# Spans of 512 queries, one ring of seven PSUM banks and a gating product on Pool, in two layers of attention with experts

## The chip, the cores and the metric

One core of a Trainium2 chip. The metric is the device time of one execution in microseconds (us); the kernel before was run three times, and one more execution was profiled. Engine names are those of the profile: PE (TensorE), DVE (VectorE), ACT (ScalarE), POOL (GpSimd), SP (SyncE, which issues the DMAs).

## What is computed

`x` is (4, 1024, 128), float32. Four residual steps follow one another, each on the layer norm of `x`:

```
x = x + attention_a(norm(x))   # 16 heads of 8; softmax over all keys, then the causal mask, no renormalising
x = x + experts(norm(x))       # softmax router over 8 experts, 2 chosen, plus one shared expert
x = x + attention_b(norm(x))   # 16 heads of 8, rotary tables, full softmax, output projection and bias
x = x + experts(norm(x))       # the same weights again
```

An expert is `(silu(h @ w1) * (h @ w3)) @ w2` with all widths 128. The kernel computes all nine experts for every token and multiplies each by its gate (zero where it was not chosen). Softmax subtracts the row's maximum, so every score is computed twice: once (queries on partitions) for the maximum, once (keys on partitions, with the negated maximum as two more rows of the contraction) for the exponent.

## The kernel before, in words

Tokens lie on partitions; a batch of 1024 tokens is two chunks of 512, a chunk four tiles of 128. Attention is cut into 32 groups: layer (0 or 2, attention a or b), batch, and a set of four heads. The four heads of a group lie at partitions 0, 32, 64 and 96, so their products with a contraction of 24 or 26 rows use different rows of PE's array.

A plan, one list of items (`make_plan`), is walked by all five engines; each engine issues its part of every item in that order and waits on semaphores. `begun` is the start: projections of chunks 0 and 1, then score units with the other six projections between them. `attention` is the loop of 1024 steps, two to a block (128 keys by 512 queries by 4 heads). A step holds, in this order: the side items due at it, one score unit 46 steps ahead (`LEAD`), two exponent products and their exponentials, and half of the weighing of the block two behind. `ended` is the rest.

- A score unit (`scores`, L1114 to L1124) is two products of 512 keys into a slot of two banks, and one DVE reduction of 128x1024 (`take_max`, L912 to L917). 32 units make a group; then `combine` (L919), a transpose, a split in two limbs on POOL (`split_max`, L610) and eight small DMAs (`load_maxima`, L513) put the maxima into `qx`. The exponents of a group wait for them.
- An exponent (`exponent`, PE L1140 to L1148, ACT L751 to L761) is one product into one bank and one ACT instruction of 128x512.
- `weigh` (L1163) multiplies the exponentials by the values, in four column groups; `mask` on POOL (L625) makes the causal diagonal blocks of attention a.
- Banks: a ring of three single banks (`ONE`) for all that ACT reads, a ring of two double slots (`TWO`) for all that DVE reads, and one bank that accumulates. `bank_of` and `slot_of` (L1058, L1065) wait until the user before in the same ring is read.
- Projections: `query_or_key` (L1098), `values` (L1106), `split_qk` (L730) and `projected_a` (L121) for attention a; `queries_keys` (L1088), `rope_product` (L891) and `projected_b` for attention b. The rows go to DRAM (`store`) and come back by group (`load`, L501, eight DMAs of 96 KB on SP).
- An expert unit (one expert, one chunk; 144 in all, `feed_forward` L148) is: h1 on PE (three products, L1201), tanh and a copy on ACT (L798, L801), silu on DVE (two operands in SBUF, L961), h3 on PE, hid on DVE (L970), y on PE (L1219), a copy on ACT (L825), four scalings and one addition on POOL (`add_gated`, L638). Units come every 7 steps (`PACE`). Those of layer 1 for a batch begin 50 steps after it is done. In `ended` the unit uses Silu on ACT (L803), one DVE pass (L974), four scalings on ACT (L816) and one addition on POOL (L660).
- Before a chunk's units stand its statistics, transpose and logits (`prepared`), and before a batch's gates a chain of 19 small DVE operations on the router's logits (`chain`), eight chains in all.

## Time and profile before

| | |
|---|---|
| three runs, median (lowest to highest) | 2003.87 us (1995.84 to 2017.19) |
| the profiled execution: its time, its span | 2010.94 us, 2009.2 us |
| busy PE / DVE / ACT / POOL | 1857.0 / 1571.9 / 1447.1 / 715.7 us |
| mean granted TensorE clock | 0.944 of full speed |
| first exponential, last exponential | 137.2 us, 1919.6 us |

The span runs from the first to the last instruction. Matmuls overlap and their ends are modelled, so PE's busy time is no measure of how full it is; the stretches, waits and intervals below are read for that.

### The profile page before, as it was taken

Reading aid. Unit: us, or ns where it says so; the run is one execution under the profiler, and the core shown is the slowest. Engines: PE = TensorE matmul, PEld = TensorE weight load, DVE = VectorE, ACT = ScalarE, POOL = GpSimd, SP = SyncE. Lnnn points to the kernel's source line nnn. Section 1 sums busy time; section 2 is a strip of 40 time slices with the busy share of each in tenths; the row PEclk is TensorE's granted clock in tenths of the full one; section 3 lists DMA queues with packets and bytes.
Section 4 is the critical chain, followed back from the end, with each engine's and each line's share of the span. In section 5 each row is a group of like instructions: output and inputs, shape, how many; then the busy total and the mean of one; then the engine's idle time right before and its main releaser. Section 6 shows DMA issues by size and latency. Waiting matters only on the chain.

```text
span 2009.2 us, 42496 instructions
## 1 busy us (share of the span) xinstructions
PE 1857.0 (92%) x16784; PEld 884.3 (44%) x16784; DVE 1571.9 (78%) x2030; ACT 1447.1 (72%) x2890; POOL 715.7 (36%) x984
## 2 busy tenths in 40 slices
PE   2889999999999999999989999999998999999988
PEld 1344443444444444444444444444444444444467
DVE  3779999988969789888888888888878888887132
ACT  1238888877667776777877787776786778778765
POOL 4222223344634446444452322323222222322244
PEclk7559999999969999999999999989999999999999
DMA  5220100000100001001010010101000000000000
GB/s 178 110 111 18 46 19 18 19 17 18 49 18 16 35 18 49 18 18 41 11 48 17 17 49 18 38 13 48 17 23 18 23 13 20 10 2 8 1 6 17
DMA packets 38087, 61.79 MB, mean 31 GB/s; under 512 B 4352, under 2 KB 19328, under 8 KB 37760
## 3 DMA queue, kind: packets, MB, share of 16 engines
q1 hardware_dynamic: 37888, 59.07, 8.3%
q8 instruction: 133, 2.18, 0.5%
q14 instruction: 66, 0.54, 0.1%
HBM read 30.74 MB, written 27.26 MB: 29 GB/s over the span
## 4 chain that ended last, share of the span: by engine, by line
PE 69%; DVE 18%; ACT 6%; issue 5%; POOL 1%; DMA 1%; SPq 0%; POOLq 0%; DVEq 0%; ACTq 0%
PE ps_sum L1181 22%; PE ps_two L1124 16%; DVE negmax L915 11%; PE ps_one L1148 5%; PE ps_one L1219 5%; PE ps_two L1201 4%; PE ps_one L1201 4%; PE ps_sum L1219 3%; DVE silu L961 2%; PE ps_sum L1201 2%; PE ps_sum L1148 2%; ACT probs L760 1%; DVE xn L935 1%; PE ps_two L1095 1%; PE ps_one L1103 1%
## 5 line engine op out<-in xcount | busy, mean ns | idle before, releaser
L915 DVE TENSOR_REDUCE negmax<-ps_two 128x2 f32<-128x1024 f32 x1024 | 1223.0, 1220 | 227.8 <-PE ps_two L1124 222.7
L760 ACT ACTIVATE probs<-ps_one 128x512 f32<-128x512 f32 x1382 | 783.0, 603 | 150.6 <-PE ps_one L1148 90.4
L1124 PE MATMUL ps_two<-kx,qx 24*128 24x512 f32 x2048 | 528.9, 518 | 71.1 <-DVE negmax L915 50.9
L1148 PE MATMUL ps_one<-qx,kx 26*128 26x512 f32 x1382 | 567.6, 505 | 6.8 <-ACT first L801 4.1
L1181 PE MATMUL ps_sum<-probs,vg 128*9 128x256 f32 (+1 forms) x6144 | 474.4, 382 | 7.1 <-ACT sums L767 5.6
L760 ACT ACTIVATE probs<-ps_sum 128x512 f32<-128x512 f32 x666 | 401.6, 603 | 91.9 <-PE ps_one L1148 68.4
L1124 PEld LDWEIGHTS ps_two<-kx,qx 24*128 24x128 f32 x2048 | 194.8, 189 | 444.3 <-DVE negmax L915 194.8
L648 POOL TENSOR_SCALAR scaled<-scaled,gates 128x128 f32<-128x128 f32 x468 | 173.6, 390 | 516.8 <-ACT scaled L825 516.6
L1148 PE MATMUL ps_sum<-qx,kx 26*128 26x512 f32 x666 | 336.1, 505 | 4.4 <-ACT first L801 3.2
L1148 PEld LDWEIGHTS ps_one<-qx,kx 26*128 26x128 f32 x1382 | 216.5, 184 | 61.9 <-ACT probs L760 33.3
L627 POOL TENSOR_TENSOR pdiag<-probs,causal 128x512 f32<-128x512 f32 x128 | 166.4, 1301 | 181.5 <-ACT probs L760 181.4
L1181 PE MATMUL ps_sum<-probs,w 128*9 128x256 f32 (+1 forms) x2560 | 186.2, 363 | 3.6 <-ACT sums L767 3.3
L1181 PEld LDWEIGHTS ps_sum<-probs,vg 128*9 128x9 f32 x6144 | 99.4, 89 | 186.0 <-issue 163.3
L652 POOL TENSOR_TENSOR x<-x,scaled 128x512 f32<-128x512 f32 x117 | 151.2, 1292 | 9.7
L1148 PEld LDWEIGHTS ps_sum<-qx,kx 26*128 26x128 f32 x666 | 122.9, 185 | 28.2 <-ACT probs L760 11.7
L961 DVE SCALAR_TENSOR_TENSOR silu<-silu,first 128x512 f32<-128x512 f32 x117 | 104.0, 889 | 22.4 <-ACT first L801 22.4
L1219 PE MATMUL ps_one<-w,hid 128*128 128x128 f32 x712 | 107.7, 297 | 5.7 <-DVE hid L974 5.7
L970 DVE TENSOR_TENSOR hid<-silu,ps_two 128x512 f32<-128x512 f32 x117 | 80.2, 685 | 40.2 <-PE ps_two L1201 37.5
L1219 PEld LDWEIGHTS ps_one<-w,hid 128*128 128x128 f32 x712 | 93.7, 203 | 38.4 <-issue 15.0
L1201 PE MATMUL ps_two<-x_hi,w_hi 128*128 128x512 f32 x144 | 71.3, 495 | 18.1 <-DVE negmax L915 17.1
L825 ACT ACTIVATE scaled<-ps_one 128x512 f32<-128x512 f32 x76 | 45.4, 598 | 56.0 <-PE ps_one L1219 54.0
L615 POOL TENSOR_SCALAR mlimbs<-turned_max 32x128 fp32r<-32x128 f32 x32 | 9.2, 288 | 205.5 <-ACT turned_max L777 205.4
(153 smaller groups left out, 1883.4 us busy)
## 6 DMA issues: line engine op xcount, KB each, us to landing
qk_rows<-limbs SPq DMA_DIRECT2D x36, 512.0 KB, 3.3
qx<-qk_rows SPq DMA_DIRECT2D x128, 96.0 KB
kx<-qk_rows SPq DMA_DIRECT2D x128, 96.0 KB
qk_rows<-prod_c SPq DMA_DIRECT2D x8, 512.0 KB, 3.7
qx<-mlimbs SPq DMA_DIRECT2D x256, 4.0 KB
qk_rows<-prod_s SPq DMA_DIRECT2D x4, 512.0 KB, 2.9
out_dram<-x SPq DMA_DIRECT2D x8, 256.0 KB, 2.3
x<-in_x SPq DMA_DIRECT2D x3, 512.0 KB, 6.1
```

The costliest lines, as they stand in the source:

```text
L627: pool.tensor_tensor(m.pdiag[:, d % 2, :, :], m.probs[:, blk % PROB_SLOTS, :, at:at + P], m.causal[:, :].unsqueeze(1).to_broadcast([P, GH, ...
L648: last = pool.tensor_scalar(part, part, m.gates[:, c * CT + t, e:e + 1], 0.0, ALU.mult, ALU.add)
L652: pool.tensor_tensor(x, x, m.scaled[:, i % 2, :], ALU.add).then_inc(s.added, 1)
L760: act.activation(m.probs[:, blk % PROB_SLOTS, EXP_HEADS[k], :], bank, ACT.Exp, scale=SCALE).then_inc(s.freed[ONE], 1)
L915: dve.tensor_reduce(m.negmax[:, unit // UNITS % 2, half, first:first + NT + 1:NT], ps.rearrange("p (h k) -> p h k", h=2), AX.X, ALU.max, n ...
L961: dve.scalar_tensor_tensor(m.silu[:, k % 2, :], m.silu[:, k % 2, :], 1.0, m.first[:, :], ALU.add, ALU.mult).then_inc(s.silued, 1)
L970: dve.tensor_tensor(m.hid[:, k % 2, :], m.silu[:, k % 2, :], ps[:, 0:CHUNK], ALU.mult).then_inc(s.freed[TWO], 1)
L1124: last = pe.matmul(slot[:, bank * CHUNK:(bank + 1) * CHUNK], m.qx[rows, n % SLOTS, i * P:(i + 1) * P], m.kx[rows, n % SLOTS, half * CHUNK: ...
L1148: pe.matmul(bank, m.kx[rows, n % SLOTS, j * P:(j + 1) * P], m.qx[rows, n % SLOTS, half * CHUNK:(half + 1) * CHUNK], start=True, stop=True) ...
L1181: last = pe.matmul(m.acc[32 * h:32 * h + width, q0 - half * CHUNK:q1 - half * CHUNK], w, src, start=j == 0 and part == 0 and k == 0, stop= ...
L1201: last = pe.matmul(dst, weights[:, w, e, :], x, start=i == 0, stop=i == 2)
L1219: last = pe.matmul(bank[:, t * D:(t + 1) * D], m.hid[:, k % 2, t * P:(t + 1) * P], m.w2[:, e, :], start=True, stop=True, skip_group_check= ...
```

## The change

1. **Spans.** Attention is walked in 64 spans of 512 queries and one group, in the order batch, half of the batch's queries, group (`place`), instead of 32 groups of 1024 queries. A chunk is done after four spans. Maxima are combined, turned, split and loaded for each span, so 64 times, with half the columns and the same number of DMAs. `LEAD` is 30 instead of 46. A batch's four groups stay in the four slots of `qx` and `kx` until the second half is done; then the next batch's group is loaded.
2. **Banks.** Seven single banks form one ring in the order of the plan, whoever reads them; an item waits for the reader of the seventh item before it. A score unit is two items with one reduction of 128x512 each; attention b's projections are four items with one rotary product of 128x512 each. In a step the exponents now stand ahead of the scores.
3. **Experts.** The copy of h1 stays on ACT, with two buffers. DVE does (tanh + 1) * h3 straight from PSUM, and POOL multiplies that by h1 (`first_into_hidden`); silu on DVE is gone. y waits for POOL. In the end stage y is an item `mix`, which DVE scales and adds to x from PSUM, four instructions a unit, without ACT and POOL.
4. **Plan.** Four projections of attention a stand in the start and four come in the loop, 16 steps apart. Layer-3 experts are prepared by chunk from chunk 4 on, the units' pace is 7 up to step 800 and 5 after it, and only the last chunk's chain is left for the end. The DMA pattern of `load` goes over rows first and the three products second.

```diff
-UNITS = NT * HALVES * 2
-BLOCKS = HALVES * NT
-EXPS = BLOCKS * GH
-TOTAL = 2 * GROUPS * UNITS
+SPANS = GROUPS * HALVES
+UNITS = CT * HALVES * 2
+TOTAL = 2 * SPANS * UNITS
-E_BANKS = 3
+BANKS = 7
-LEAD = 46
+LEAD = 30
-PACE = 7
+PACE, LATE_PACE, LATE_FROM = 7, 5, 800
-RING = {"turn": ONE, "q": ONE, "k": ONE, "v": ONE, "logits": ONE, "h1": ONE, "y": ONE, "exp": ONE, "oturn": ONE, "omix": ONE,
-        "qk": TWO, "scores": TWO, "h3": TWO}
+SCALAR, VECTOR = "read by ScalarE", "read by VectorE"
+READER = {"turn": SCALAR, "q": SCALAR, "k": SCALAR, "v": SCALAR, "logits": SCALAR, "h1": SCALAR, "y": SCALAR,
+          "exp": SCALAR, "oturn": SCALAR, "omix": SCALAR, "maxima": SCALAR, "sums": SCALAR,
+          "qk": VECTOR, "scores": VECTOR, "h3": VECTOR, "mix": VECTOR}
...
+def place(p):
+
+    layer, of_layer = divmod(p, SPANS)
+    b, of_batch = divmod(of_layer, NG * HALVES)
+    half, g = divmod(of_batch, NG)
+    return layer * GROUPS + b * NG + g, half
+
...
     return staged(at, (0, ("stats", 0, c)), (1, ("moments", 0, c)), (4, ("apply", 0, c)), (6, ("turn", 0, c)),
-                  (6, ("q", 0, c)), (7, ("k", 0, c)), (7, ("low", 0, c)), (7, ("store", 0, c)), (8, ("v", 0, c)))
+                  (7, ("q", 0, c)), (9, ("k", 0, c)), (9, ("low", 0, c)), (9, ("store", 0, c)), (11, ("v", 0, c)))
...
-    return staged(at, (0, ("h1", k)), (2, ("silu", k)), (4, ("h3", k)), (6, ("y", k)), (8, ("gate", k)))
+    return staged(at, (0, ("h1", k)), (3, ("h3", k)), (4, ("hidden", k)), (7, ("y", k)), (9, ("gate", k)))
...
+def woven():
+    side = {110: [("bweights",)]}
+    for c in range(CT, CHUNKS):
+        add_side(side, projected_a(c, 6 + 16 * (c - CT)))
+    ready, of_chunk = [], NG * UNITS
+    for b in range(B):
+        more, at = routed(1, b * HALVES, HALVES, (b + 1) * HALVES * of_chunk + 11)
+        add_side(side, more)
+        ready += [at] * HALVES
+    for c in range(CHUNKS - 1):
+        at = (CHUNKS + c + 1) * of_chunk + 9
+        add_side(side, mixed_heads(c, at))
+        width = HALVES if c < CHUNKS // 2 else 1
+        if (c + 1) % width == 0:
+            more, at = routed(3, c + 1 - width, width, at + 8 - 3 * (width - 1))
+            add_side(side, more)
+            ready += [at] * width
+    free = 0
+    for chunk, at in enumerate(ready):
+        for e in range(NE):
+            free = max(free, at)
+            if free + 9 >= TOTAL:
+                break
+            add_side(side, feed_forward(chunk * NE + e, free))
+            free += PACE if free < LATE_FROM else LATE_PACE
+        if chunk < CHUNKS:
+            add_side(side, projected_b(chunk, free + 14))
+    for p in range(2 * SPANS - 1):
+        add_side(side, {(p + 1) * UNITS + 2 * WEIGH_LAG + 3: [("sums", p)]})
...
 def scores_of(unit):
-    items = [("scores", unit)]
+    items = [("scores", unit, i) for i in range(2)]
     if unit % UNITS == UNITS - 1:
...
-    for n in range(2 * GROUPS):
-        add_side(side, {(n + 1) * UNITS + TURN_AT + 1 - LEAD: [("maxima", n)]})
+    for p in range(2 * SPANS):
+        add_side(side, {(p + 1) * UNITS + TURN_AT + 1 - LEAD: [("maxima", p)]})
     for step in range(TOTAL):
         blk, part = divmod(step, 2)
-        n = blk // BLOCKS
-        if step % UNITS == 0 and n and n + SLOTS - 1 < 2 * GROUPS:
-            items.append(("load", n + SLOTS - 1))
+        if step % UNITS == 0 and step:
+            n, half = place(step // UNITS - 1)
+            if half == HALVES - 1 and n + SLOTS < 2 * GROUPS:
+                items.append(("load", n + SLOTS))
         items += side.get(step, [])
-        if step + LEAD < TOTAL:
-            items += scores_of(step + LEAD)
         for k in range(2):
             items.append(("exp", blk, part * 2 + k))
             whole = blk + 1 - WEIGH_LAG
             if part and not k and whole > 0 and whole % NT == 0:
-                items.append(("copy", *divmod(whole // NT - 1, HALVES)))
+                items.append(("copy", whole // NT - 1))
+        if step + LEAD < TOTAL:
+            items += scores_of(step + LEAD)
         if part and diagonal(blk):
             items.append(("mask", blk))
...
+    plan = []
+    for first in range(0, CT, 2):
+        pair = range(first, first + 2)
+        plan += [(kind, 0, c) for c in pair for kind in ("stats", "moments")]
+        plan += [("apply", 0, c) for c in pair]
+        plan += [(kind, 0, c) for c in pair for kind in ("turn", "q", "k", "low", "store")]
+        plan += [("v", 0, c) for c in pair]
+        plan += [("load", 0)] if not first else [("wsplit",), ("load", 1)]
+    side = {6: [("load", 2)], 16: [("load", 3)], UNITS + TURN_AT + 1: [("maxima", 0)]}
...
+    units = list(range(done, 2 * LAYER_UNITS))
+    late = len(units) - NE
+    stages = [[("oturn", c)], [("omix", c), ("oadd", c)], [("stats", 3, c), ("moments", 3, c), ("apply", 3, c)],
+              [("turn", 3, c)], [("logits", 3, c)], [("chain", 3, c, 1, k) for k in range(CHAIN)]]
+    side = {}
+    for i, stage in enumerate(stages):
+        add_side(side, {1 + i * (late - 1) // len(stages): stage})
...
-        items += [("y", k), ("gate", k)]
+        items.append(("mix", k))
...
+    def bank(self, *item):
+        return self.ring[item] % BANKS
+    def held_by(self, *item):
+        i = self.ring[item] - BANKS
+        return self.order[i] if i >= 0 else None
...
-    ps_one = ctx.enter_context(nc.psum_tensor("ps_one", [P, 2, CHUNK], F32))
-    ps_two = ctx.enter_context(nc.psum_tensor("ps_two", [P, 2, 2 * CHUNK], F32))
-    ps_sum = ctx.enter_context(nc.psum_tensor("ps_sum", [P, 2, CHUNK], F32))
-    m.one = (ps_one[:, 0, :], ps_one[:, 1, :], ps_sum[:, 1, :])
-    m.two = (ps_two[:, 0, :], ps_two[:, 1, :])
-    m.acc = ps_sum[:, 0, :]
+    ps_banks = ctx.enter_context(nc.psum_tensor("ps_banks", [P, BANKS, CHUNK], F32))
+    ps_sum = ctx.enter_context(nc.psum_tensor("ps_sum", [P, CHUNK], F32))
+    m.banks = tuple(ps_banks[:, i, :] for i in range(BANKS))
+    m.acc = ps_sum[:, :]
...
-                             m.qk_rows[b, i, :, g * GR + h:(g + 1) * GR:GH, :].bitcast(F32)
+                             m.qk_rows[b, i, :, g * GR + h:(g + 1) * GR:GH, :].rearrange("c r s -> r c s").bitcast(F32)
...
+    def first_into_hidden(k):
+        pool.wait_ge(s.freed[VECTOR], counts.use("h3", k) + 1)
+        pool.wait_ge(s.freed[SCALAR], counts.use("h1", k) + 1)
+        pool.tensor_tensor(m.hid[:, k % 2, :], m.hid[:, k % 2, :], m.first[:, k % 2, :], ALU.mult
+                           ).then_inc(s.hidden, 1)
...
-        if ("silu", k) in counts.kind["silu"]:
+            act.wait_ge(s.freed[VECTOR], counts.use("h3", k - 2) + 1)
+        if ("hidden", k) in counts.kind["hidden"]:
             act.activation(m.silu[:, k % 2, :], bank, ACT.Tanh, scale=0.5)
-            if k:
-                act.wait_ge(s.silued, k)
-            act.activation(m.first[:, :], bank, ACT.Copy).then_inc(s.freed[ONE], 1)
+            if k >= 2:
+                act.wait_ge(s.hidden, k - 1)
+            act.activation(m.first[:, k % 2, :], bank, ACT.Copy).then_inc(s.freed[SCALAR], 1)
         else:
-            act.activation(m.silu[:, k % 2, :], bank, ACT.Silu).then_inc(s.silu_act, 1)
-            act.wait_ge(s.silu_act, k + 1 - len(counts.kind["silu"]))
-            act.sem_inc(s.freed[ONE], 1)
-
...
+    def take_max(unit, k):
+        bank = take(("scores", unit, k))
+        i, half = divmod(unit % UNITS // 2, HALVES)
+        col = heads_of(unit)[k] * CT + i
+        dve.tensor_reduce(m.negmax[:, unit // UNITS % 2, half, col:col + 1], bank, AX.X, ALU.max, negate=True
+                          ).then_inc(s.freed[VECTOR], 1)
...
-    def silu(k):
-        dve.wait_ge(s.freed[ONE], counts.use("h1", k) + 1)
-        dve.scalar_tensor_tensor(m.silu[:, k % 2, :], m.silu[:, k % 2, :], 1.0, m.first[:, :], ALU.add, ALU.mult
-                                 ).then_inc(s.silued, 1)
     def gated_hidden(k):
-        ps = take(("h3", k))
+        bank = take(("h3", k))
         if k >= 2:
-            dve.wait_ge(s.filled[ONE], counts.use("y", k - 2) + 1)
-        if ("silu", k) in counts.kind["silu"]:
-            dve.wait_ge(s.silued, k + 1)
-            dve.tensor_tensor(m.hid[:, k % 2, :], m.silu[:, k % 2, :], ps[:, 0:CHUNK], ALU.mult
-                              ).then_inc(s.freed[TWO], 1)
+            tail = ("mix", k - 2) in counts.kind["mix"]
+            done = ("mix", k - 2) if tail else ("y", k - 2)
+            dve.wait_ge(s.filled[READER[done[0]]], counts.use(*done) + 1)
+        dve.wait_ge(s.freed[SCALAR], counts.use("h1", k) + 1)
+        if ("hidden", k) in counts.kind["hidden"]:
+            dve.scalar_tensor_tensor(m.hid[:, k % 2, :], m.silu[:, k % 2, :], 1.0, bank, ALU.add, ALU.mult
+                                     ).then_inc(s.freed[VECTOR], 1)
         else:
-            dve.wait_ge(s.silu_act, k + 1 - len(counts.kind["silu"]))
-            dve.scalar_tensor_tensor(m.hid[:, k % 2, :], m.silu[:, k % 2, :], 2.0, ps[:, 0:CHUNK], ALU.mult, ALU.mult
-                                     ).then_inc(s.freed[TWO], 1)
+            dve.scalar_tensor_tensor(m.hid[:, k % 2, :], m.silu[:, k % 2, :], 2.0, bank, ALU.mult, ALU.mult
+                                     ).then_inc(s.freed[VECTOR], 1)
+    def add_mixed(k):
+        bank = take(("mix", k))
+        layer, c, e = ffn_unit(k)
+        dve.wait_ge(s.gated, counts.chains[(layer, c)] + 1)
+        dve.wait_ge(s.constants, 1)
+        dve.wait_ge(s.added, counts.added_before(("mix", k), plan))
+        i = counts.nth("mix", k)
+        if i:
+            dve.wait_ge(s.mixed, i)
+        for t in range(CT):
+            tile = c * CT + t
+            x = m.x[:, tile_cols(tile)]
+            last = dve.scalar_tensor_tensor(x, bank[:, t * D:(t + 1) * D], m.gates[:, tile, e:e + 1], x,
+                                            ALU.mult, ALU.add)
+        last.then_inc(s.mixed, 1)
+        dve.wait_ge(s.mixed, i + 1)
...
 
-        count = counts.use(*item)
-        if count >= E_BANKS:
-            pe.wait_ge(s.freed[ONE], count - E_BANKS + 1)
-        return m.one[count % E_BANKS]
-
-    def slot_of(item):
-
-        count = counts.use(*item)
-        if count >= 2:
-            pe.wait_ge(s.freed[TWO], count - 1)
-        return m.two[count % 2]
+        holder = counts.held_by(*item)
+        if holder:
+            pe.wait_ge(s.freed[READER[holder[0]]], counts.use(*holder) + 1)
+        return m.banks[counts.bank(*item)]
...
+    def mix_experts(kind, k):
         e = k % NE
-        pe.wait_ge(s.freed[TWO], counts.use("h3", k) + 1)
+        if ("hidden", k) in counts.kind["hidden"]:
+            pe.wait_ge(s.hidden, k + 1)
+        else:
```

## Rows read from the trace of the kernel before

**Rows 1.** The page's head: busy time, share and instructions; shares of the ending chain.

```profile
PE 1857.0 (92%) x16784; PEld 884.3 (44%) x16784; DVE 1571.9 (78%) x2030; ACT 1447.1 (72%) x2890; POOL 715.7 (36%) x984
...
PE 69%; DVE 18%; ACT 6%; issue 5%; POOL 1%; DMA 1%; SPq 0%; POOLq 0%; DVEq 0%; ACTq 0%
```

**Rows 2.** Stretches: us, PE, PEld, DVE, ACT, POOL busy (count), PE clock, DMA share, GB/s.

```profile
0.00:137.20 137.20, 82.77 (x226) 37.93 (x226) 82.82 (x152) 29.46 (x75) 44.71 (x54) 0.59 0.43 146
137.20:1921.40 1784.20, 1701.51 (x16129) 783.32 (x16129) 1457.13 (x1805) 1363.13 (x2665) 628.93 (x895) 0.97 0.06 23
1921.40:2009.20 87.80, 72.70 (x430) 63.02 (x430) 31.97 (x74) 54.51 (x151) 42.10 (x35) 0.93 0.03 10
```

**Rows 3.** The same view: four spans without expert units, two spans with them.

```profile
181.10:263.60 82.50, 81.08 (x1011) 36.23 (x1010) 76.64 (x75) 71.41 (x139) 23.80 (x24) 1.00 0.11 38
...
1649.10:1701.90 52.80, 52.32 (x464) 23.66 (x460) 44.55 (x48) 41.88 (x82) 11.54 (x22) 1.00 0.07 22
```

**Rows 4.** Stretches, exponentials (L760) alone: two to a step, so 32 steps.

```profile
1649.10:1701.90 52.80, 33.64 (x64) 1.00 0.07 22
```

**Rows 5.** Timeline of PE (start us, length): a step without scores; y; h1.

```profile
1914.25 0.49 PE L1148 MATMUL ps_one<-qx,kx 26*128 26x512 f32 x1
...
1915.23 0.69 PE L1148 MATMUL ps_one<-qx,kx 26*128 26x512 f32 x2
...
1677.08 1.16 PE L1219 MATMUL ps_one<-w,hid 128*128 128x128 f32 x8
1678.17 0.50 PE L1124 MATMUL ps_two<-kx,qx 24*128 24x512 f32 x2
...
1679.15 0.50 PE L1201 MATMUL ps_one<-x_hi,w_hi 128*128 128x512 f32 x1
...
1680.04 0.50 PE L1124 MATMUL ps_two<-kx,qx 24*128 24x512 f32 x2
```

**Rows 6.** Waits in 1649.1 to 1701.9: us in total, times, longest.

```profile
ACT probs L760 <- PE ps_one L1148: 5.1, 5, 1.6
PEld ps_two L1124 <- DVE negmax L915: 3.2, 8, 0.6
...
PEld ps_two L1201 <- DVE negmax L915: 2.0, 4, 0.7
PEld ps_two L1124 <- DVE hid L970: 1.7, 4, 0.4
PEld ps_one L1148 <- ACT probs L760: 1.5, 5, 0.3
```

**Rows 7.** Timeline of the start: first scores, three reductions in a row, SP's issues of maxima.

```profile
38.89 0.80 PE L1124 MATMUL ps_two<-kx,qx 24*128 24x512 f32 x4 [18.66 <-DMA kx<-qk_rows]
...
74.35 3.48 DVE L915 TENSOR_REDUCE negmax<-ps_two 128x2 f32<-128x1024 f32 x3
...
119.69 5.83 SPq L519 DMA_DIRECT2D qx<-mlimbs  x8
```

**Rows 8.** The page's groups: busy us, mean ns of one, idle before and its releaser.

```profile
L915 DVE TENSOR_REDUCE negmax<-ps_two 128x2 f32<-128x1024 f32 x1024 | 1223.0, 1220 | 227.8 <-PE ps_two L1124 222.7
...
L648 POOL TENSOR_SCALAR scaled<-scaled,gates 128x128 f32<-128x128 f32 x468 | 173.6, 390 | 516.8 <-ACT scaled L825 516.6
...
L652 POOL TENSOR_TENSOR x<-x,scaled 128x512 f32<-128x512 f32 x117 | 151.2, 1292 | 9.7
...
L961 DVE SCALAR_TENSOR_TENSOR silu<-silu,first 128x512 f32<-128x512 f32 x117 | 104.0, 889 | 22.4 <-ACT first L801 22.4
...
L970 DVE TENSOR_TENSOR hid<-silu,ps_two 128x512 f32<-128x512 f32 x117 | 80.2, 685 | 40.2 <-PE ps_two L1201 37.5
```

**Rows 9.** Timeline of the end: the last sums, the first product of two successive units.

```profile
1921.40 0.60 ACT L767 ACTIVATE sums<-ps_sum 128x512 f32<-128x512 f32 x1 [1.24 <-PE ps_sum L1181]
...
1979.39 0.48 PE L1201 MATMUL ps_sum<-x_hi,w_hi 128*128 128x512 f32 x1
...
1981.67 0.48 PE L1201 MATMUL ps_one<-x_hi,w_hi 128*128 128x512 f32 x1
```

473 lines of the change are left out of this document (213 added, 260 removed).

## Prediction

> **What bounds the kernel now.** I read the page's busy line first: PE 92% of the span, DVE 78%, ACT 72%, and the chain that ended last is 69% PE and 18% DVE [rows 1]. A busy PE is not a full one, so I cut the span at the first and the last exponent instruction [rows 2]. The start (137.2 us) has ACT busy for only 29.5 us: nothing is exponentiated yet. The loop takes 1784.2 us for 1024 steps and 117 expert units. The end (87.8 us) has 27 units and an idle DVE. Each stage has its own limit.
>
> In the loop I compare equal stretches [rows 3, 4]. Four spans of 16 steps without expert units take 82.5 us, so 20.6 each, with DVE busy 76.6: DVE is nearly full there. Two spans of 16 steps with units (pace 7, so 2.29 units a span) take 52.8 us, so 26.4 each, or 2.5 us for a unit. There DVE is busy for 44.6 and ACT for 41.9 of 52.8, and PE's queue is what fills the time. Unhindered, PE needs 0.98 us from one step's exponents to the next, 1.09 us for a unit's mixing product, 0.89 us for each hidden product [rows 5]: 16 x 0.98 + 2.29 x 2.87 + about 0.6 of turned sums and maxima = 22.9 of 26.4. The missing 3.5 us are stalls: PE's queue waited for DVE 3.2 + 2.0 + 1.7 us and for ACT 1.5 us in two spans, and while it did, ACT sat idle for exponents for 5.1 us [rows 6]. The loop is bound by PE plus coupling through the banks.
>
> **The sum, part by part**, against the profiled execution (span 2009.2, execution 2010.94).
>
> *Start, -63.* Before, 46 units of scores with six projections between them run ahead of the first exponent. Scores begin at 38.9, after PE waited 18.7 us for the first group's load [rows 7]. After, two more projections stand ahead of the scores, inside that wait (PE is idle in it; their DMAs are queued behind the load of group 0), and only 30 units follow. Each is now two reductions of 512. Three reductions of 1024 back to back took 3.48 us and one alone 1.22 [rows 7, 8], so the interval is 1.13, 0.06 above 1.067 (1024 elements at the rate between the two sizes: a 128x512 pass from PSUM takes 0.685, a 128x1024 one 1.220 [rows 8], 0.535 for 512). A half then takes 0.596, a step 1.19: 30 x 1.19 = 36, so exponents start at about 75. The maxima of span 0 leave after unit 19, at 62; their eight DMAs take 5.8 us to issue [rows 7], 9 us in all with transpose and split, so they land near 71 and hide. If the second pair of projections delays the scores, exponents start at 84; if the reordered load lands sooner, at 70. The reordered pattern costs nothing that I can read; the wait of 18.7 bounds what it can give.
>
> *Four projections move into the loop, +18.* In the start stage 137.2 - 38.9 = 98.3 us less 46 x 1.13 = 52 leaves 46 us for six, 7.7 each, at a mean granted clock of 0.59 [rows 2]. At 0.97 in the loop about 4.5 each. Ends 3 and 7.7.
>
> *Steps without units, +5.* DVE per span: 16 x (1.19 - 1.13) = +1.0, partly in its 8% idle time. Ten such spans (steps 0 to 165) at +0.5.
>
> *Spans with units, -80.* DVE loses the silu pass (mean 0.889 [rows 8]) and keeps one hidden pass of 0.69: -0.889 x 2.29 = -2.0 a span against +1.0 for the split reductions. More important to me is that the exponents now go ahead of the scores: PE's wait for DVE comes after ACT has been fed. An exponent could reach back 3 uses of its banks, now 7 of all, of which about four belong to one step. So the depth in steps hardly grows (1.5 to 1.75 for exponents, 2 to 1.75 for scores); only a unit's h1 and y, which took one of three banks, take one of seven. Of the 4.2 us a span that PE waits in all (8.4 in two [rows 6]) I take 1.5 as gone. Ends: 0 (DVE only a little lighter, depth alike) and 3.5 (all stalls). There are 53 spans with units: 53 x 1.5 = 80. The product moved to Pool takes 1.29 us [rows 8] and lies between h3 and y, four steps (about 6 us) apart; Pool is busy 629 of 1784 us in the loop [rows 2], plus 129 x 1.29 = 166, so it hides, unless it stands behind a gate (4 x 0.39 + 1.29) and a mask in Pool's queue.
>
> *Twelve more units in the loop, +24.* In the new plan the gates of layer 3's chunks 0 and 1 are ready at step 680, of 2 and 3 at 808, and later ones in time: 18 units at pace 7 from 680 to 806, 18 at pace 5 from 808 to 898, 18 more to 988, then three of chunk 6 from step 1000. With layer 1's 72 that makes 129 in the loop, and 15 remain. Each costs 2.0 us where the average was 2.5. Ends 1.5 and 2.9.
>
> *Maxima, chains and chunk 6, +23.* 64 combines, transposes and splits instead of 32: 32 x 0.4 = 13 (ends 5 and 20; the eight DMAs stay eight each, so SP issues 32 x 5.8 us more, beside other work, as it has 11 steps for them). Two router chains more and chunk 6's mixing and preparation, which were in the end stage: 10.
>
> *End, -38.* Before, the steady unit takes 2.28 us (1979.39 to 1981.67), so 27 units would take 62 of the 87.8 us from the last sums on [rows 2, 9]; the other 26 are the way to the last batch's gates and the drain. After, one chunk's chain (copy, turn, mix, statistics, transpose, logits, 19 small DVE operations) beside six units: I add up some 26 us to the gates, then 9 x 2.28 = 21, then 3 to drain, since the last product goes from PSUM to x on DVE without ACT and Pool: 50 instead of 87.8. Ends 44 and 60.
>
> Sum: -63 + 18 + 5 - 80 + 24 + 23 - 38 = -111, so 1898 in span and 1900 in execution. The profiled execution lies 7 us above the median of 2003.87, inside the runs' 1995.84 to 2017.19; I predict 1893 for the median.
>
> **Rivals.**
> 1. *The ring gives nothing in the loop.* Its depth in steps is the same, and one bank now serves both readers, so a late DVE also holds ACT's banks. Then only the ends gain: 1893 + 80 = 1973. For it: the depths above. Against it: the order of exponents and scores, and silu's 104 us gone.
> 2. *PE's own time is reached.* All of the 3.5 us a span goes: 53 x (3.5 - 1.5) = 106 less, 1787. For it: ACT and DVE have 20% and 16% spare in those stretches. Against it: the masked layer has longer weighing, and pace 5 is denser.
> 3. *Slower: the fixed part of 1024 more reductions decides.* Alone, a reduction of 1024 takes 1.220, so 0.153 above 1.067. If each half pays that, a step costs DVE 1.373 instead of 1.131: +3.9 us a span, less 2.0 of silu where there are units. With the same stalls: 1973 + 53 x 1.9 + 10 x 3.4 + 7 = 2115. It decides from 31 us over rival 1, 0.03 us a step; with the 80 us saved, from 0.11 us a step. Against it: the interval of 1.13 [rows 7] shows only 0.06 exposed when work is waiting. The Trainium skill, VectorE: DVE Perf Modes, section "Side-by-side: where the cycles go", gives every instruction some 150 cycles of init and decode beside its elements, about 0.156 us; by that rule, were it paid one after the other, a step's two halves would take 2 x 662 / 0.96 = 1.379 us and this rival would hold, at about the same time. The row of three in 3.48 us speaks against paying it in a full queue.
> 4. *Pool stands on the path.* y waits for Pool's product; behind a gate of 2.9 us or a rotation PE would stand still. At 0.8 us a unit, 129 x 0.8 = 103: 1996, no change to be seen.
>
> **How the numbers follow.** Forecast 0.50, its own range 1855 to 1935. Rival 1 0.18, rival 2 0.20, rival 3 0.06, rival 4 0.06. About 1% (20 us) is what this measurement can tell. Faster by over 1%, below 1984: 0.50 + 0.20 + 0.15 + 0.01 = 0.86; within 1%: 0.03 + 0.04 = 0.07; slower 0.07. The range leaves out the far part of rival 2 and rivals 3 and 4: 1810 to 1975.
>
> **What would show it.** First exponent between 70 and 84; last sums some 50 us before the end; 128x512 reductions near 0.69 alone and 0.60 apart; in a span with units, DVE's waits on PE's queue below 2.5 us; no wait of PE's y for Pool over 0.3 us in the mean. Wrong if the plain span is over 22 us (rival 3), if the span with 2.29 units stays at 26 (rival 1) or falls below 23.5 (rival 2).

## The result, and the profile after

The changed kernel takes 1905.56 us (median of four runs, 1903.06 to 1907.96), the kernel before, run beside it, 2006.59 us (1995.84 to 2017.19). The ratio is 0.9496, its 95% interval 0.9465 to 0.9527: faster by 5%, 101 us. The forecast was 1893 and its own range 1855 to 1935. Some executions run at a lower granted clock and take some per cent longer: every ratio here leaves them out, the medians and ranges keep them.

The page's head of the changed kernel, against [rows 1]:

```profile
PE 1852.5 (97%) x16816; PEld 885.6 (47%) x16816; DVE 1566.8 (82%) x3083; ACT 1432.9 (75%) x2840; POOL 883.0 (46%) x1210
...
PE 86%; DVE 9%; ACT 2%; issue 2%; POOL 1%; DMA 0%; DVEq 0%; ACTq 0%; POOLq 0%
```

Busy times are almost what they were (PE 1857.0, DVE 1571.9); only POOL rose, by 167 us. What changed is the chain that ended last: PE's share is 86% where it was 69, DVE's 9 where it was 18.

The three stages cut as in [rows 2], then three plain spans to set against the four of [rows 3], one quiet span with two units, and spans 10 to 41, counted from 0, as one stretch (columns as in [rows 2]):

```profile
0.00:71.00 71.00, 52.92 (x127) 26.46 (x127) 44.70 (x110) 15.25 (x39) 29.92 (x42) 0.77 0.60 193
71.00:1849.90 1778.90, 1758.05 (x16452) 823.46 (x16451) 1488.62 (x2865) 1401.29 (x2777) 849.29 (x1164) 0.99 0.08 27
1849.90:1904.10 54.20, 41.56 (x238) 35.70 (x238) 33.44 (x109) 16.37 (x26) 3.81 (x4) 0.91 0.04 11
199.20:261.70 62.50, 61.98 (x761) 28.33 (x759) 60.03 (x106) 53.60 (x106) 18.92 (x21) 1.00 0.20 63
...
656.30:681.90 25.60, 25.60 (x273) 12.31 (x271) 22.10 (x38) 21.09 (x42) 15.01 (x21) 1.00 0.10 33
...
315.40:1230.60 915.20, 902.10 (x8621) 428.55 (x8620) 780.58 (x1490) 713.29 (x1409) 497.48 (x663) 1.00 0.09 28
```

The start is 66.2 us shorter, the loop 5.3, the end 33.6: 105 in all. A plain span takes 20.8 us (before 20.6), the quiet span with units 25.6. The same view of the kernel before, first the quiet span of layer 1 that answers to the one above, then its spans 10 to 41 of 16 steps:

```profile
708.10:735.30 27.20, 26.93 (x308) 13.82 (x306) 22.92 (x23) 21.17 (x41) 11.31 (x15) 1.00 0.07 27
...
352.60:1302.20 949.60, 898.26 (x8581) 421.17 (x8580) 804.84 (x1015) 705.85 (x1383) 404.85 (x549) 0.97 0.07 27
```

So 32 spans with the same exponents and about as many units (72, before 70) were 34.4 us shorter, 1.1 each. The mean clock column reads 0.97 before and 1.00 after; by the clock records, TensorE stood at the lower level (1.2 of 2.4 GHz) for 48.8 us of the one stretch and 3.4 us of the other. At half the rate these 45 us are worth up to 23 of the 34.4 (an estimate that takes PE as busy all through).

The reductions and Pool's product in the page's groups (columns as in [rows 8]), and the start's reductions in the timeline (start, length, as in [rows 7]):

```profile
L940 DVE TENSOR_REDUCE negmax<-ps_banks 128x1 f32<-128x512 f32 x2048 | 1280.7, 680 | 196.0 <-PE ps_banks L1153 192.4
...
L680 POOL TENSOR_TENSOR hid<-hid,first 128x512 f32<-128x512 f32 x129 | 164.9, 1278 | 125.8 <-DVE hid L991 121.4
...
L991 DVE SCALAR_TENSOR_TENSOR hid<-silu,ps_banks 128x512 f32<-128x512 f32 x129 | 88.1, 683 | 29.1 <-PE ps_banks L1232 23.9
```

```profile
37.45 12.65 DVE L940 TENSOR_REDUCE negmax<-ps_banks 128x1 f32<-128x512 f32 x21 [9.46 <-PE ps_banks L1153]
```

One reduction of 512 takes 0.680 us, but 21 in a row take 12.65: they start 0.598 apart, (12.65 - 0.68) / 20. The forecast had 0.685 and 0.596.

### The profile page after: what moved, and what is told of

Same layout as the page of the kernel before. It is cut to its first block, busy times and chain, and to the rows that moved or that the text cites. A ratio compares the mean times of both kernels' runs of the same rounds, so it can differ in the third digit from the quotient of the medians.

```text
span 1904.1 us, 44343 instructions
## 1 busy us (share of the span) xinstructions
PE 1852.5 (97%) x16816; PEld 885.6 (47%) x16816; DVE 1566.8 (82%) x3083; ACT 1432.9 (75%) x2840; POOL 883.0 (46%) x1210
## 4 chain that ended last, share of the span: by engine, by line
PE 86%; DVE 9%; ACT 2%; issue 2%; POOL 1%; DMA 0%; DVEq 0%; ACTq 0%; POOLq 0%
PE ps_sum L1212 28%; PE ps_banks L1178 20%; PE ps_banks L1232 11%; PE ps_banks L1153 9%; PE ps_banks L1253 8%; DVE negmax L940 5%; PE ps_banks L1124 2%; PE ps_banks L1167 2%; PE ps_banks L1131 1%; DVE xn L958 1%; PE ps_banks L1110 1%; PE ps_banks L1223 1%; ACT sums L810 1%; PE ps_banks L1138 1%; PE ps_banks L1160 1%
## 5 line engine op out<-in xcount | busy, mean ns | idle before, releaser
L940 DVE TENSOR_REDUCE negmax<-ps_banks 128x1 f32<-128x512 f32 x2048 | 1280.7, 680 | 196.0 <-PE ps_banks L1153 192.4
L803 ACT ACTIVATE probs<-ps_banks 128x512 f32<-128x512 f32 x2048 | 1085.7, 604 | 195.2 <-PE ps_banks L1178 182.5
L1153 PE MATMUL ps_banks<-kx,qx 24*128 24x512 f32 x2048 | 650.0, 507 | 7.4 <-DVE hid L991 3.6
L1178 PE MATMUL ps_banks<-qx,kx 26*128 26x512 f32 x2048 | 528.6, 500 | 3.5 <-DVE hid L991 1.8
L1178 PEld LDWEIGHTS ps_banks<-qx,kx 26*128 26x128 f32 x2048 | 197.3, 183 | 374.1 <-issue 168.1
L1153 PEld LDWEIGHTS ps_banks<-kx,qx 24*128 24x128 f32 x2048 | 260.4, 185 | 103.6 <-ACT probs L803 55.1
L680 POOL TENSOR_TENSOR hid<-hid,first 128x512 f32<-128x512 f32 x129 | 164.9, 1278 | 125.8 <-DVE hid L991 121.4
L1253 PE MATMUL ps_banks<-w,hid 128*128 128x128 f32 x1152 | 167.9, 290 | 5.7 <-DVE hid L994 3.9
L1253 PEld LDWEIGHTS ps_banks<-w,hid 128*128 128x128 f32 x1152 | 143.5, 194 | 55.3 <-issue 46.3
L1232 PE MATMUL ps_banks<-x_hi,w_hi 128*128 128x512 f32 x288 | 143.7, 499 | 0.1
```

The costliest lines, as they stand in the source:

```text
L680: pool.tensor_tensor(m.hid[:, k % 2, :], m.hid[:, k % 2, :], m.first[:, k % 2, :], ALU.mult).then_inc(s.hidden, 1)
L803: act.activation(m.probs[:, blk % PROB_SLOTS, EXP_HEADS[k], :], bank, ACT.Exp, scale=SCALE).then_inc(s.freed[SCALAR], 1)
L940: dve.tensor_reduce(m.negmax[:, unit // UNITS % 2, half, col:col + 1], bank, AX.X, ALU.max, negate=True).then_inc(s.freed[VECTOR], 1)
L1153: pe.matmul(bank_of(("scores", unit, k)), m.qx[rows, n % SLOTS, tile * P:(tile + 1) * P], m.kx[rows, n % SLOTS, half * CHUNK:(half + 1) * ...
L1178: pe.matmul(bank, m.kx[rows, n % SLOTS, j * P:(j + 1) * P], m.qx[rows, n % SLOTS, half * CHUNK:(half + 1) * CHUNK], start=True, stop=True) ...
L1232: last = pe.matmul(dst, weights[:, w, e, :], x, start=i == 0, stop=i == 2)
```

## The experiments

All ratios are to the kernel before, run beside it on the same chip; the changed kernel stands at 0.9496. Each kernel has one profile. This table gives, for the 32 spans 10 to 41, their length and the time in them at the lower clock level by the records; both come from that one profile:

```
kernel                             median us   spans 10-41   of it at 1.2 GHz
before                               2006.6        949.6        48.8
changed                              1905.6        915.2         3.4
scores ahead of exponents            2023.1        991.6       105.8
two rings of single banks            1946.4        945.3        51.2
banks and reductions of before       1945.1        945.2        34.1
  the same, scores ahead             1951.9        937.8        30.7
before, exponents ahead              2034.1        966.6        61.2
silu on DVE                          1939.9        935.4        30.7
projected first                      1908.5        920.3        17.1
woven items last                     1916.3        916.7        44.4
woven items in the middle            2120.5       1045.3       187.7
six banks                            2117.2       1014.2        63.9
late pace 7                          1904.1        924.5        27.3
late pace 6                          1898.6        918.5        13.7
```

The last two rows say how far one profile can be trusted. Their plan differs from that of the changed kernel only from step 800 (span 50) on, so in spans 10 to 41 they do the same work in the same order; yet the stretch took 915.2, 918.5 and 924.5 us. Differences of some 10 us in this column, and of some 25 us in the last, show nothing. The row of the woven items in the middle comes from the longest of that kernel's six executions and is too high for its median.

### Scores ahead of exponents again

```diff
         items += side.get(step, [])
+        if step + LEAD < TOTAL:
+            items += scores_of(step + LEAD)
         for k in range(2):
             items.append(("exp", blk, part * 2 + k))
...
-        if step + LEAD < TOTAL:
-            items += scores_of(step + LEAD)
```

> The changed kernel (1905.6 us) with one part undone: in a step the score unit stands ahead of the exponents again. Theory (the order matters: PE's wait for DVE comes after ACT has been fed): spans with units grow by 0.5 to 0.9 us, the run by 30 to 50 us, to 1935 to 1955, and ACT's waits for exponents on PE grow. Rival (the order in a step is nothing, the ring's depth is what it is either way): within 5 us of the changed kernel.

Measured: 2023.14 us (2013.21 to 2055.62), ratio 1.0089, interval 1.005 to 1.0129. With the old order the new kernel loses its whole gain and more, 118 us. The chain and the waits of that run (us in total, times, longest):

```profile
PE 70%; DVE 18%; issue 5%; ACT 4%; POOL 2%; DMA 0%; DVEq 0%; POOLq 0%; ACTq 0%
```

```profile
ACT probs L803 <- PE ps_banks L1178: 257.4, 365, 14.5
...
PEld ps_banks L1178 <- DVE negmax L940: 125.7, 271, 2.5
PEld ps_banks L1153 <- DVE negmax L940: 112.5, 276, 1.0
```

and the same waits of the changed kernel:

```profile
ACT probs L803 <- PE ps_banks L1178: 182.5, 242, 13.4
PEld ps_banks L1178 <- issue: 168.1, 461, 0.8
PEld ps_banks L1178 <- DVE negmax L940: 85.9, 200, 1.1
```

The chain is back at the shares of [rows 1]. PE's exponents (L1178) wait 40 us longer for a reduction and ACT 75 us longer for PE. The largest rise is at PE's scores (L1153), 112.5 us of waiting for a reduction, which in the changed kernel is this row:

```profile
PEld ps_banks L1153 <- DVE negmax L940: 27.5, 86, 1.1
```

### The ring cut in two, and the banks of before

Two rings: `bank` gives `use % 3` to what ACT reads and `3 + use % 4` to what DVE reads, and `held_by` looks three or four uses back among the same reader's items:

```diff
-        return self.ring[item] % BANKS
+        return self.use(*item) % 3 if READER[item[0]] == SCALAR else 3 + self.use(*item) % 4
```

> The changed kernel with its seven banks cut into two rings, three for what ACT reads and four single ones for what DVE reads. Theory (one ring helps because h1 and y take one bank of seven and not one of three): 15 to 40 us slower, with more waits of PE for ACT in spans with units, and plain spans unchanged near 20.9 us. Rival (the depth in steps is the same, 1.5 and 2 against 1.75, so one ring gives nothing): within 5 us.

Measured: 1946.44 us (1938.64 to 1968.85), ratio 0.9705, interval 0.9667 to 0.9744. The split costs 41 us. It costs none of that in plain spans, as the view of three of them shows (20.9 us each), and 30 us in spans 10 to 41:

```profile
311.50:1256.80 945.30, 911.29 (x8624) 428.63 (x8620) 781.78 (x1489) 717.61 (x1409) 497.96 (x663) 0.97 0.08 27
199.10:261.70 62.60, 61.93 (x762) 27.89 (x759) 60.12 (x106) 53.90 (x107) 18.97 (x21) 1.00 0.20 62
```

The waits of PE's exponents say where it goes; the first three rows are of the two rings, the last three of the one:

```profile
PEld ps_banks L1181 <- ACT probs L806: 200.5, 555, 0.8
...
PEld ps_banks L1181 <- ACT first L848: 63.2, 93, 1.0
PEld ps_banks L1181 <- ACT scaled L857: 33.1, 86, 0.7
```

```profile
PEld ps_banks L1178 <- ACT probs L803: 69.6, 183, 0.8
...
PEld ps_banks L1178 <- ACT scaled L854: 7.6, 21, 0.4
PEld ps_banks L1178 <- ACT first L845: 2.7, 6, 0.5
```

With three banks for ACT an exponent waits until ACT has copied an h1 (`first`) or a y (`scaled`), 96 us in all against 10, and until it has read an earlier exponent, 200 against 70. In the one ring its exponents wait for DVE instead, 86 us for reductions and 26 for `hid`, which the two rings don't have; the sum is still smaller. That is the reason the forecast gave for the ring: h1 and y take one bank of seven and not one of three.

The second kernel goes further back: three banks and two double slots, with one reduction over both banks of a slot:

```diff
-        dve.tensor_reduce(m.negmax[:, unit // UNITS % 2, half, col:col + 1], bank, AX.X, ALU.max, negate=True
-                          ).then_inc(s.freed[VECTOR], 1)
+        dve.tensor_reduce(m.negmax[:, unit // UNITS % 2, half, col:col + CT + 1:CT],
+                          m.pairs[:, first * CHUNK:(first + 2) * CHUNK].rearrange("p (h k) -> p h k", h=2), AX.X,
+                          ALU.max, negate=True).then_inc(s.freed[VECTOR], 2)
```

> The changed kernel with the banks of the kernel before: ring of three for ACT, two double slots for DVE, reductions of 128x1024. It differs from the run with two rings by the size of the reductions only. Theory (a half costs DVE 0.60 us against 0.565 for its share of a whole one, 66 us in all, partly in DVE's idle time): 10 us faster to 5 us slower than the two rings, plain spans at 20.5. Rival (the fixed part of 1024 more instructions is on the path): at least 30 us faster than the two rings.

Measured: 1945.07 us (1940.70 to 1979.02), ratio 0.9705, interval 0.9667 to 0.9744. Halving the reductions costs nothing that can be seen, 1 us against the run above, though DVE's busy time differs:

```profile
L963 DVE TENSOR_REDUCE negmax<-ps_pairs 128x2 f32<-128x1024 f32 x1024 | 1223.2, 1220 | 284.1 <-PE ps_pairs L1177 276.9
```

1223.2 us of reductions here, 1280.7 in the changed kernel: 57 us more busy time that costs nothing. Rival 3 is refuted.

### Order and banks, crossed

The order of before with the banks of before, in the changed kernel (both edits above together):

> The changed kernel with both of the earlier choices together: three banks for ScalarE and two joined pairs for VectorE with 1024-wide reductions, and the scores planned ahead of the exponents. Apart, the banks cost 40 us and the order 118. If the order is dear only in the single ring, where a score bank is handed over behind a product's or a bank of the other reader, this run lies at 1945 to 1985. If the two costs add up, it lies near 2060. The first would say that ring and order must be changed together.

Measured: 1951.93 us (1942.13 to 1970.96), ratio 0.9735, interval 0.9692 to 0.9778. The order is worth 7 us between the medians with separate rings, within the spread (the intervals overlap), and 118 in one ring. The two costs don't add up: in the changed kernel the order matters only with the one ring.

The kernel before with the exponents ahead of the scores, nothing else:

```diff
         items += side.get(step, [])
-        if step + LEAD < TOTAL:
-            items += scores_of(step + LEAD)
         for k in range(2):
             items.append(("exp", blk, part * 2 + k))
...
+        if step + LEAD < TOTAL:
+            items += scores_of(step + LEAD)
```

> The kernel before with one line moved: in each step the exponents of the block are planned ahead of the scores four units on, as the changed kernel does; two rings, three joined reductions, stages and loads stay as they were. If the order by itself carries the gain, the loop comes down to the 1780 us of the changed kernel with more than its work in it: 1880 to 1920 in all. If the order only matters where one ring serves both readers (the changed kernel with the scores ahead lost 118 us), it is worth under 1%: 1985 to 2010 here.

Measured: 2034.14 us (2026.18 to 2042.62), ratio 1.0133, interval 1.0101 to 1.0166. It is 1.3% slower, clear of the interval, which neither expectation held. The order that the single ring needs costs 26 us here and nothing that can be seen in the changed kernel with the same banks; which other part of the change makes that difference is open. Its waits beside those of before: DVE for scores 262.4 us against 222.7; PE's scores for DVE only 54.7 against 194.8; PE's exponents, now first in the step, for ACT's reading of their three banks 197.3 against 45.0; ACT for exponents 243.0 against 225.0 (one of the three banks lies in `ps_sum`, so these are sums of two rows).

```profile
DVE negmax L915 <- PE ps_two L1124: 262.4, 329, 28.6
...
ACT probs L760 <- PE ps_one L1148: 157.7, 155, 3.3
PEld ps_one L1148 <- ACT probs L760: 137.9, 378, 1.2
...
ACT probs L760 <- PE ps_sum L1148: 85.3, 82, 2.7
```

### Where the woven items stand

```diff
-        items += side.get(step, [])
         for k in range(2):
             items.append(("exp", blk, part * 2 + k))
...
         if step + LEAD < TOTAL:
             items += scores_of(step + LEAD)
+        items += side.get(step, [])
```

> The changed kernel with one line moved: the woven items of a step (projections, routing, experts) are planned behind its exponents and scores instead of ahead of them. Putting scores ahead of exponents cost 118 us with ScalarE's wait for TensorE's exponent products up from 182 to 257 us, so whatever stands ahead of the exponents seems to be paid there. If that is the mechanism, the wait falls again, by 30 to 80 us, and the time by 10 to 40: 1865 to 1895. If the place of the woven items only shifts the same wait to their own readers, 1900 to 1915; slower if VectorE's part of them comes later and holds banks of the ring, 1920 to 1960.

Measured: 1916.32 us (1915.08 to 1920.69), ratio 0.9547, interval 0.9519 to 0.9575. Eleven us above the changed kernel, whose slowest run (1907.96) lies below the fastest one here: no gain, and ACT's wait rose to 254.4 us where I had it fall. That the exponents' place in the step alone decides is refuted. Some spans got shorter (span 13 took 24.7 against 27.2, span 15 29.7 against 33.0), others longer (span 17 took 35.3 against 30.0).

```profile
ACT probs L803 <- PE ps_banks L1178: 254.4, 351, 13.4
```

The same with the line between exponents and scores:

> The changed kernel with the woven items between a step's exponents and its scores. ScalarE gets its two exponent products first, as in the run with the woven items last, but VectorE gets the items' banks before its maxima. If only what stands ahead of the exponents counts, this equals the run with the woven items last (within 10 us); if the scores' place counts as well, the two differ, this one being between it and the changed kernel or slower than both.

Measured: 2120.52 us (2094.51 to 2183.13), ratio 1.0479, interval 1.0436 to 1.0522. Here ACT waits 508.9 us for exponents. The profiled execution (2183.13) is the longest of the six, so its rows overstate what the others did.

```profile
PEclk8699966899999999899898997799879996886799
...
ACT probs L803 <- PE ps_banks L1178: 508.9, 577, 13.4
```

These four orders fall in two classes. Read as a circle, the ring's users come as exponents, scores, woven items in the changed kernel and with the woven items last (1906 and 1916), and as scores, exponents, woven items in the other two (2023 and 2121). In the first class the woven items follow the scores in the ring, in the second the exponents. What is the same within a class is who inherits whose bank; I did not test the circle itself further.

### Six banks

```diff
-BANKS = 7
+BANKS = 6
```

> The changed kernel with six banks in its one ring, the seventh left unused. Cutting the seven into three and four cost 41 us. If what the ring gives is slack between a bank's reader and its next writer, one bank fewer takes a seventh of it from everyone: 1915 to 1960. If six are as good as seven, 1902 to 1910, then the number of banks was never scarce and the two rings lose by their split alone. Over 1960 would say that the ring stands at an edge, where every bank decides.

Measured: 2117.20 us (2103.18 to 2123.17), ratio 1.0529, interval 1.0481 to 1.0577: one bank is worth 212 us. Now the plain spans suffer too, 24.1 us each against 20.8, at the full clock level:

```profile
225.80:298.00 72.20, 69.88 (x763) 30.79 (x760) 62.36 (x106) 54.95 (x105) 18.94 (x22) 1.00 0.17 54
```

```profile
PEld ps_banks L1153 <- ACT probs L803: 8.7, 22, 1.1
...
PEld ps_banks L1178 <- DVE negmax L940: 7.0, 21, 0.4
```

The second fence is the waits of these three spans. A step takes four banks, so seven and six banks differ in whom an item waits for. Counting back in the plan (e exponent, s score, the digit its number in the step):

```
order and banks       waits for the reader of, steps back
e0 e1 s0 s1, seven    e0: e1, 2   e1: s0, 2   s0: s1, 2   s1: e0, 1
e0 e1 s0 s1, six      e0: s0, 2   e1: s1, 2   s0: e0, 1   s1: e1, 1
s0 s1 e0 e1, seven    s0: s1, 2   s1: e0, 2   e0: e1, 2   e1: s0, 1
```

With six banks both scores wait for ACT's reading of the step before, the row L1153 for L803 above, which in the three plain spans of the changed kernel comes to 0.9 us in 3 waits; the exponents' wait for DVE, two steps back, rose as well (7.0 us, against 1.3). My count of the forecast ("1.5 to 1.75 steps") took the mean of these reaches, and six banks change it only from 1.75 to 1.5.

The table alone does not explain the order. With the scores ahead, the item that reaches one step back is an exponent that waits for a reduction. In three plain spans of that run (21.6 us each) this wait is 0.7 us; what grew is a score's wait for a reduction two steps back, which the same view of the changed kernel does not have at all:

```profile
PEld ps_banks L1153 <- DVE negmax L940: 11.2, 31, 0.4
...
PEld ps_banks L1178 <- DVE negmax L940: 0.7, 3, 0.2
```

So whom an item waits for, and how late that reader is when PE comes to the item, both count, and why the order costs 118 us in the one ring stays open.

### Silu back on DVE

```diff
-            dve.scalar_tensor_tensor(m.hid[:, k % 2, :], m.silu[:, k % 2, :], 1.0, bank, ALU.add, ALU.mult
+            dve.wait_ge(s.hidden, k + 1)
+            dve.tensor_tensor(m.hid[:, k % 2, :], m.silu[:, k % 2, :], bank, ALU.mult
                                      ).then_inc(s.freed[VECTOR], 1)
```

and (tanh + 1) * h1 as one more DVE instruction two steps after h1; POOL's product is gone.

> The changed kernel with the product of tanh and first half of the experts' gate taken from Pool to VectorE (129 operations of about 0.69 us, 89 us of VectorE time; Pool loses 129 of 1.28 us). If VectorE stands beside the path as my forecast had it (each unit 0.3 to 0.5 us dearer), 1935 to 1975; if Pool's product is only an off-path move, no change, 1900 to 1912; if the chain Pool to TensorE was itself late, faster than 1895.

Measured: 1939.85 us (1934.48 to 1943.72), ratio 0.9669, interval 0.9641 to 0.9697. The move to Pool is worth 34 us, within the first case. Quiet spans are as long as in the changed kernel (25.6); spans 10 to 41 take 20 us more in this profile (11 more than with pace 7, whose plan there is the changed kernel's), and span 43 36.9 against 31.8. DVE's group for it:

```profile
L983 DVE SCALAR_TENSOR_TENSOR silu<-silu,first 128x512 f32<-128x512 f32 x129 | 101.2, 784 | 7.2 <-ACT first L843 7.0
```

101 us of DVE's time cost 34 us of the kernel's.

### All projections ahead of the loop

```diff
-    for c in range(CT, CHUNKS):
-        add_side(side, projected_a(c, 6 + 16 * (c - CT)))
...
     side = {6: [("load", 2)], 16: [("load", 3)], UNITS + TURN_AT + 1: [("maxima", 0)]}
+    for c in range(CT, CHUNKS):
+        add_side(side, projected_a(c, 6 * (c - CT)))
```

> The changed kernel with chunks 4 to 7 normalized, turned and projected before the first scores, as the kernel before has it. The four spans that carry a projection now (25.5 to 30.0 us against 20.9 for plain ones) should come down to about 21, so the loop loses some 20 us; the start grows. If the start grows by the whole difference to the kernel before (66 us) the sum is 1945 to 1960; if the chunks are only as dear in the start as they are in the loop, no change, 1900 to 1915.

Measured: 1908.47 us (1906.20 to 1913.65), ratio 0.9519, interval 0.9491 to 0.9547: 3 us, within the spread. Start and loop of this run:

```profile
0.00:92.00 92.00, 59.01 (x193) 29.35 (x193) 60.78 (x165) 29.13 (x74) 44.34 (x54) 0.73 0.62 210
92.00:1857.10 1765.10, 1746.46 (x16386) 817.42 (x16385) 1478.14 (x2810) 1390.17 (x2741) 837.48 (x1152) 0.98 0.07 24
```

The start grows by 21 us, the loop falls by 14. Weaving the projections in moved time and gained almost none. The other 45 us by which the new start is shorter than the old one I put down to the shorter lead, the half-sized first maxima and the loads; I took none of these apart.

### The pace of the late experts

```diff
-PACE, LATE_PACE, LATE_FROM = 7, 5, 800
+PACE, LATE_PACE, LATE_FROM = 7, 7, 800
```

> The changed kernel with pace 7 to the end of the loop instead of pace 5 from step 800: 120 units in the loop and 24 in the end, instead of 129 and 15. Theory (read from the changed kernel's spans: at pace 5 a unit more costs (29.7 - 25.7) / 0.91 = 4.4 us, in the end stage 2.3, and more units cover the last chunk's chain): loop 30 to 40 us shorter, end 10 to 20 us longer, run 10 to 25 us faster. Rival (a unit costs 2.0 in the loop as I forecast, and 2.3 in the end): 0 to 5 us slower.

Measured: 1904.07 us (1901.70 to 1912.35), ratio 0.9509, interval 0.9477 to 0.9542: no difference. And at pace 6:

> The changed kernel with the late pace at 6 in place of 5 (7 gave no change: 1904): of the 144 expert units fewer stand in the late spans and more in the end, where TensorE waits some 28 us for the last chunk's routing and each unit costs 2.3 us. My sum says a unit in the late spans costs over 4 us, so some six moved ones give 8 to 15 us: 1890 to 1900. The rival, from the run at pace 7: nothing within 4 us, since the loop loses its moved units' price but meets other stalls.

Measured: 1898.59 us (1885.69 to 1909.10), ratio 0.9460, interval 0.9422 to 0.9499. Its stages, and its last fourteen spans beside those of the changed kernel:

```profile
69.30:1827.30 1758.00, 1736.91 (x16396) 813.66 (x16395) 1482.35 (x2861) 1396.68 (x2764) 834.64 (x1140) 0.99 0.08 27
1827.30:1888.80 61.50, 49.44 (x294) 42.87 (x294) 40.70 (x129) 18.78 (x30) 3.82 (x4) 0.97 0.05 14
1453.80:1825.30 371.50, 367.53 (x3267) 171.88 (x3271) 295.47 (x578) 310.42 (x613) 165.13 (x255) 1.00 0.05 13
```

```profile
1454.00:1848.00 394.00, 390.76 (x3327) 183.42 (x3330) 301.75 (x581) 314.83 (x625) 179.65 (x279) 1.00 0.05 13
```

Four units (125 Pool products instead of 129) left those spans, which shrank by 22.5 us, and the end grew by 7.3. This profile (1888.8) is of one of the kernel's shorter executions, 8 us under its median. At pace 7 the loop (1766.0) is 12.9 below the changed kernel's, though its spans 10 to 41 took 9 us longer in that profile, and the end (72.2) 18.0 above. The interval of pace 6 overlaps that of the changed kernel, so no version here is shown to beat it; its median is 7 us lower.

## Why the prediction was right, step by step

The sum was -111 in span, and -105 came. The stages fit: start -63 forecast, -66.2 measured; loop -10, -5.3; end -38, -33.6. Inside the loop the terms fit less well, and their errors cancelled.

- *Start, -63.* Reductions 0.596 apart, measured 0.598; first exponent at 75, measured 71.0. Right; that the lead and the halved reductions account for it is not taken apart.
- *Four projections, +18.* The first four spans took 106.6 us, before 85.2: +21.4. With the projections first they took 86.3, so their price in the loop was 20.3, 5.1 each for 4.5 (4.8 in the three spans that lie wholly at the full clock level). Right. What the forecast didn't say is that the start pays 21 for them too, so that their move gains nothing.
- *Steps without units, +5, and Maxima, chains and chunk 6, +23.* In plain spans the first of these terms and the doubled maxima of the second were to add 0.5 and 0.2 us a span; together they added 0.2 to 0.3, and next to nothing when the joined reductions came back (20.7 a span there). Right, a little high. The chains and chunk 6's part, 10 of the 23, no run prices.
- *Spans with units, -80.* The size was near, the place and the weight of the reasons were not. I expected 1.5 us off each span alike. Quiet span 14 went from 27.2 to 25.6, quiet spans 46 and 47 only from 26.4 and 26.5 to 26.2 and 26.0, and spans 10 to 41 lost 1.1 each; part of the gain sits in the clock. DVE's waits on PE's queue in span 14 came to 1.8 us, below the 2.5 that I had named. The 8.4 us that I took for all of PE's waits in two spans left out 1.7 us of y for DVE and 1.0 us of the weighing for ACT. By the experiments the loop owes about 40 us to the ring (given the new order), for the reason given, and 34 to Pool's product; that these two come to 74 beside a forecast of 80 is in part luck, since I had named the order as the main reason. The step that failed is the reason "more important to me is that the exponents now go ahead of the scores": by itself that order made the kernel before 1.3% slower, and with separate rings it gives 7 us, within the spread. It is not a gain of its own but the condition under which one ring pays; without it the ring turns from 40 us of gain into 71 of loss (2023 against 1952).
- *Twelve more units, +24.* Not settled. I priced a late unit at 2.0 us, with ends 1.5 and 2.9. Spans 50 to 63 hold 40 units, before 30, and took 394.7 us to the last exponential against 384.2, with the other gains in them. At pace 7 the last fourteen spans took 372.9 with nine units fewer, 21.1 less, 2.3 each, with 10.2 us of it at the lower clock. At pace 6 four units fewer gave 22.5 less, 5.6 each, above my upper end; from there to pace 7 five more gave nothing. So a price per unit does not describe these spans: how dense they stand seems to count, and each of these numbers rests on one profile. At 2.3 the twelve would cost 28.
- *End, -38.* The gates came 28 us after the last sums (forecast 26), then nine units at 2.29. Right; the wait before the first of the nine, and its clock, it lacked. The last DVE instruction of the chain and the first mixing products after it:

```profile
1877.74 0.19 DVE L1066 TENSOR_TENSOR gates<-room 128x32 f32<-128x32 f32 x1
```

```profile
1878.93 2.07 PE L1253 MATMUL ps_banks<-w,hid 128*128 128x128 f32 x8 [3.24 <-DVE hid L994]
...
1886.24 1.05 PE L1253 MATMUL ps_banks<-w,hid 128*128 128x128 f32 x8
...
1888.53 1.05 PE L1253 MATMUL ps_banks<-w,hid 128*128 128x128 f32 x8
```

PE had waited 3.24 us, and the first eight products then took 2.07 us where the later ones take 1.05: the clock was at its lower level until about 1884.

- *Rival 1* (the ring gives nothing): refuted by the two rings, +41; its sign, a span with 2.29 units that stays at 26, was nearly met (25.6), so the span alone would not have decided it. *Rival 2* (PE's own time reached): the quiet span stayed at 25.6, above its mark of 23.5. *Rival 3*: refuted, as told; of a reduction's 0.680 us, 0.08 is hidden where the next one is waiting. The 150 cycles of the Trainium skill that I weighed there (VectorE: DVE Perf Modes, section "Side-by-side: where the cycles go for N=2048 bf16") would give 0.69 us between two reductions of 512 if each paid them in turn. The trace shows 0.598 between two and 0.680 for one, so the figure fits the length of one and not the interval of many. *Rival 4* (Pool on the path): refuted, putting the product back on DVE made the kernel slower, and in the changed kernel's waits y's weight loads waited for Pool four times in 129 units (and its products four times, 1.6 us in all):

```profile
PEld ps_banks L1253 <- POOL hid L680: 3.0, 4, 0.9
```

## What to carry to other kernels

A ring of buffers shared by two engines is judged by its waits, item by item: one bank less cost 212 us and another order 118, while the mean reach moved from 1.75 steps to 1.5 or not at all. Writing down which reader each item waits for, and how many steps back, is a start, but the waits of a plain stretch decide: here they named another item than the one with the shortest reach. Change the ring and the order of its users together, and test each alone in both settings; putting the exponents first gained 118 us in one ring of seven, nothing that can be seen with the rings of before in the changed kernel, and cost 26 in the kernel before. Shorter instructions or fewer busy microseconds of an engine that has work queued are worth little by themselves: 57 us of reductions were free, and 101 us of DVE's products cost 34. And profile the same plan more than once before a difference of 10 us in a stretch is read.

## What the runs showed of the hardware that I had not expected

The granted clock differs between executions that do the same work, and the time with it. In spans 10 to 41 the changed kernel stood at the lower level for 3.4 us; the kernels with late pace 6 and 7, which have the same plan there, for 13.7 and 27.3 us, and the stretch was 3.3 and 9.3 us longer. With the scores ahead it was 105.8 us and the stretch 76.4 us longer. If PE were busy all through, the lower level would account for half of the added low-clock time, 51 of 76 (an estimate); the rest is the stalls themselves. It is not a fixed relation: with the woven items last the stretch had 41 us more at the lower level and was only 1.5 us longer, and six banks had 60 us more and 99. So part of what looks like the price of a wait can be the clock's. That the stalls bring the lower level is likely from the large cases, but no run here isolates it.

A row of reductions is quicker than its parts: one of 128x512 takes 0.680 us, and 21 in a row start 0.598 us apart.
